# A redesigned order for a gated attention and mixture-of-experts block, without filler products

## The reference

```python
x = x + tanh(g_xattn[0]) * xattn(layernorm(x), ctx_768, Wq, bq, Wkv, bkv, Wo, bo)    # 16 heads of 8
x = x + tanh(g_ffn[0]) * ffn(layernorm(x), Wg, bg, W1, b1, W2, b2)
# ffn: cur = x (2048 tokens); for r in range(4):
    logits = flat @ Wg[r] + bg[r]
    vals, idx = jax.lax.top_k(logits, 2)          # of 4 experts
    w = jax.nn.softmax(vals, axis=-1)
    hmid = jax.nn.gelu(jnp.einsum('nh,ehf->enf', flat, W1) + b1[:, None, :])   # f = 512
    y = jnp.einsum('enf,efh->enh', hmid, W2) + b2[:, None, :]
    cur = cur + einsum('ne,enh->nh', cw, y)       # cw: w at the chosen experts, 0 elsewhere
```

## Time and profile before

| | |
|---|---|
| three runs, us | 505.62 (median), 504.99, 509.12 |
| profiled execution, us | 505.52 |
| its span, us | 503.7 |
| TensorE busy | 479.5 us, 95% of the span |
| VectorE, ScalarE, GpSimd busy | 74%, 75%, 16% |
| chain that ended last | 83% TensorE, 8% VectorE, 3% ScalarE |
| mean granted clock of TensorE | 0.993 |

### The profile page before, as it was taken

One profiled execution on the slowest core, in us unless ns is written; L12 is line 12 of the kernel. 1 busy time (PEld: TensorE's weight loads), 2 busy tenths in 40 slices (PEclk: granted clock), 3 DMA queues, 4 the chain that ended last, 5 costly groups with the idle time before them and its releaser, 6 DMA issues.

```text
span 503.7 us, 9018 instructions
## 1 busy us (share of the span) xinstructions
PE 479.5 (95%) x2977; PEld 385.5 (77%) x2977; DVE 374.3 (74%) x741; ACT 375.9 (75%) x757; POOL 83.1 (16%) x132
## 2 busy tenths in 40 slices
PE   4798998999999999999999999999999999999995
PEld 3567776777887878888888888888888888888884
DVE  5449587888879687866977697778669776877775
ACT  2457576776969687887878788878878877888773
POOL 5736298673220000000000000000000000000000
PEclk9999799999999999999999999999999999999999
DMA  5900000001302020040031004000400130050001
GB/s 145 320 29 7 10 3 14 2 15 32 139 1 85 0 85 2 3 167 1 1 115 55 0 2 169 1 0 3 167 1 0 44 128 1 0 191 0 21 1 42
DMA packets 15156, 25.20 MB, mean 50 GB/s; under 512 B 3490, under 2 KB 11527, under 8 KB 13063
## 3 DMA queue, kind: packets, MB, share of 16 engines
q1 hardware_dynamic: 11136, 22.05, 12.3%
q0 software_dynamic: 2592, 2.10, 2.3%
q10 hardware_dynamic: 1382, 0.49, 0.4%
HBM read 22.82 MB, written 1.18 MB: 48 GB/s over the span
## 4 chain that ended last, share of the span: by engine, by line
PE 83%; DVE 8%; issue 4%; ACT 3%; DMA 1%; ACTq 1%; DVEq 0%
PE ps L1215 11%; PE ps L1217 11%; PE ps L1216 11%; PE ps L1202 11%; PE ps L1204 11%; PE ps L1203 11%; PE ps L1117 4%; PE ps L1105 3%; PE ps L1133 2%; PE ps L1138 2%; DVE least L800 1%; PE ps L1177 1%; DVE rT_sb L816 1%; PE ps L1176 1%; ACT g_sb L724 1%
## 5 line engine op out<-in xcount | busy, mean ns | idle before, releaser
L851 DVE TENSOR_TENSOR h_lo<-g_sb,h_hi 128x512 fp32r<-128x512 f32 x256 | 170.1, 688 | 78.1 <-ACT h_hi L731 78.1
L724 ACT ACTIVATE g_sb<-ps,cols 128x512 f32<-128x512 f32 x256 | 174.8, 686 | 68.1 <-PE ps L1204 67.8
L731 ACT ACTIVATE h_hi<-g_sb 128x512 fp32r<-128x512 f32 x256 | 154.1, 631 | 0.0
L1215 PE MATMUL ps<-h_hi,w_hi 128*128 128x512 f32 x256 | 103.1, 403 | 0.0
L1217 PE MATMUL ps<-h_hi,w_lo 128*128 128x512 f32 x256 | 101.2, 395 | 0.0
L1202 PE MATMUL ps<-x_hi,w_hi 128*128 128x512 f32 x256 | 101.1, 395 | 0.0
L1216 PE MATMUL ps<-h_lo,w_hi 128*128 128x512 f32 x256 | 101.0, 394 | 0.0
L1204 PE MATMUL ps<-x_hi,w_lo 128*128 128x512 f32 x256 | 100.1, 391 | 0.0
L1203 PE MATMUL ps<-x_lo,w_hi 128*128 128x512 f32 x256 | 99.8, 390 | 0.0
L1217 PEld LDWEIGHTS ps<-h_hi,w_lo 128*128 128x128 f32 x256 | 48.0, 188 | 11.9
L1204 PEld LDWEIGHTS ps<-x_hi,w_lo 128*128 128x128 f32 x256 | 48.0, 188 | 11.3
(11 more groups left out here) (122 smaller groups left out, 480.0 us busy)
## 6 DMA issues: line engine op xcount, KB each, us to landing
cwb_even<-cw_rows SPq DMA_DIRECT2D x8, 1024.0 KB, 5.0
cwb_odd<-cw_rows SPq DMA_DIRECT2D x8, 1024.0 KB, 4.7
w_hi<-in_L_ffn_W_dram POOLq DMA_DIRECT2D x2, 1024.0 KB, 9.1
x_sb<-in_x_dram SPq DMA_DIRECT2D x4, 256.0 KB, 5.2
w_in<-in_L_ffn_W_dram SPq DMA_DIRECT2D x1, 1024.0 KB, 6.2
out_dram<-xn SPq DMA_DIRECT2D x4, 256.0 KB, 2.3
ctx_sb<-in_ctx_dram ACTq DMA_DIRECT2D x4, 115.5 KB
v_st<-v_sb SPq DMA_DIRECT2D x8, 38.5 KB
```

The source lines that it names most:

```text
L724: nc.scalar.activation(g_sb[:, k, :], ps[:, k, :], ACT.Gelu_apprx_tanh, bias=b1_c[:, e * NF + k:e * NF + k + 1]).then_inc(gelu_done, 1)
L731: nc.scalar.activation(h_hi[:, u % 2, k, :], g_sb[:, k, :], ACT.Copy).then_inc(hi_done, 1)
L851: nc.vector.tensor_tensor(h_lo[:, u % 2, k, :], g_sb[:, k, :], h_hi[:, u % 2, k, :].bitcast(F32), ALU.subtract).then_inc(lo_done, 1)
L1215: mm(yb, w2_hi[:, w], hh, start=k == 0, stop=False)
```

## The change

Six things change. Shown are the parts that decide an order; the rest follows from them.

The router's logits of the six paired routes are made from the other side: the router weights are now the stationary operand (`wg_w`: four copies of high and low part in 32-column groups, made once by VectorE in batch 3), x moves past them in four products of 512 columns (`wide_logits`), ScalarE copies the 8 useful rows of each group to `lgs` (`move_logits`), and one unit later two transposes bring them to tokens by columns. Ranking, weights and transposed weights come one unit later, the gate in the same unit as before.

```diff
         LOGITS_AT = {1: 2, 5: 3}
         ROUTER_AT = {2: 2, 6: 3}
         GATE_AT = {2: 2, 6: 3}
         WEIGHTS_AT = {3: 2, 7: 3}
-        CWT_AT = {4: 2, 8: 3}
-        MOVE_AT = {4: 2, 8: 3}
+        CWT_AT = {5: 2, 8: 3}
+        MOVE_AT = {5: 2, 8: 3}
         for q in range(NC, len(ROUTES)):
             u = 2 * E * (q - NC + 1)
-            LOGITS_AT[u + 1] = q
-            ROUTER_AT[u + 2] = q
+            WIDE_AT[u + 1] = q
+            LOGITS_AT[u + 2] = q
+            ROUTER_AT[u + 3] = q
             GATE_AT[u + 3] = q
-            WEIGHTS_AT[u + 3] = q
-            CWT_AT[u + 5] = q
-            MOVE_AT[u + 5] = q
+            WEIGHTS_AT[u + 4] = q
+            CWT_AT[u + 6] = q
+            MOVE_AT[u + 6] = q
...
+            def wide_logits(q):
+
+                pe.wait_ge(wg_split, 4)
+                pe.wait_ge(x_split, ROUTES[q][-1] + 1)
+                pe.wait_ge(gate_step, GATE_OPS * (q - 1) + 2)
+                pe.wait_ge(cwT_moved, q)
+                wg = wg_w[:, ROUTES[q][0] // NC, :, :].rearrange("p t w -> p (t w)")
+                for n, i in enumerate(ROUTES[q]):
+                    mm(ps[:, 6 + n, :], wg, x_hi[:, i % NC, :], start=True, stop=False)
+                    m = mm(ps[:, 6 + n, :], wg, x_lo[:, i % NC, :], start=False, stop=True)
+                m.then_inc(lgw_done, 1)
+
+            def transpose_logits(q):
+
+                k = 32 * (TC - 1) + 2 * E
+                pe.wait_ge(lgw_moved, q - NC + 1)
+                for n in range(2):
+                    m = tr(ps[:, 6, n * P:n * P + k], lgs[0:k, n, :], ident[0:k, 0:k])
+                m.then_inc(logits_done, 1)
+
...
+            def move_logits(q):
+
+                act.wait_ge(lgw_done, q - NC + 1)
+                act.wait_ge(zero_done, 2)
+                if q > NC:
+                    act.wait_ge(logits_done, q - 2)
+                for t in range(TC):
+                    rows = slice(32 * t, 32 * t + 2 * E)
+                    m = nc.scalar.activation(lgs[rows, :, :], ps[rows, 6:8, t * P:(t + 1) * P], ACT.Copy)
+                m.then_inc(lgw_moved, 1)
+
```

At the start the first chunk is split into a part "a" (batch 0) and "b" (batches 1 to 3), the low and high K of batch 0 are made on VectorE (`stage_k0`), and GpSimd issues its two large loads ahead of the inverse deviations. TensorE, VectorE and GpSimd:

```diff
-            transpose_xn(0)
+            transpose_xn("a")
             moved(pe, "W")
             project_k(0)
             moved(pe, "W")
+            project_q("a")
+            moved(pe, "W")
             project_v(0)
+            scores(0, 0)
+            scores(0, 1)
+            transpose_xn("b")
             moved(pe, "W")
-            project_q(0)
+            project_q("b")
             pe.wait_ge(bv_wide, 1)
             mm(bank("BO")[:, 0:D], bv_w[:, :], wT[:, 3, :], start=True, stop=True).then_inc(job_mm, 1)
-            scores(0, 0)
-            scores(0, 1)
...
-            moments(0, 0)
             dve.wait_ge(c_ready, 2)
             nc.vector.tensor_reduce(head_mask[:, :], head_at[:, :, :].rearrange("p q h -> p h q"), AX.X,
                                     ALU.add).then_inc(headmask_ready, 1)
-            normalise(0)
-            moments(0, 1)
-            normalise(1)
+            moments(0, "a")
+            normalise("a")
+            moments(0, "b")
+            stage_k0()
             moved(dve, "COLS")
-            low_q(0)
+            low_q("a")
+            normalise("b")
             smallest(0, 0)
             shift(0)
+            moments(0, 1)
             smallest(0, 1)
+            moved(dve, "COLS")
+            low_q("b")
+            normalise(1)
...
-            rstd_of(0, 0)
-            rstd_of(0, 1)
+            pool.wait_ge(headmask_ready, 1)
             pool.dma_start(w1_hi[:, :].rearrange("h (e f) -> h e f", e=E),
                            W1.rearrange("e h f -> h e f")).then_inc(w_hi, 16)
             pool.dma_start(w2_hi[:, :].rearrange("p (e k h) -> p e k h", e=E, k=NF),
                            W2.rearrange("e (k p) h -> p e k h", p=P)).then_inc(w_hi, 16)
-            pool.wait_ge(headmask_ready, 1)
-            stage_k(0)
+            rstd_of(0, "a")
+            rstd_of(0, "b")
             stage_k(1)
+            rstd_of(0, 1)
```

```diff
-        NORMALISE = {3: 2, 7: 3}
+        NORMALISE = {4: 2, 8: 3}
...
                     smallest(b + 1, 0)
+                if c < NC and r == R_LOW:
+                    low_q(c)
                 if b + 1 < B:
                     shift(b + 1)
                 if b >= 2:
                     normalise_o(b - 2)
-                if b == ROUTER1_SLOT:
-                    router(1)
-                if c < NC and r == R_LOW:
-                    low_q(c)
+                if b in SPLIT_X:
+                    split_x(SPLIT_X[b])
                 if b == ROUTER0_SLOT:
                     router(0)
-                if b + 1 < B:
-                    smallest(b + 1, 1)
                 if b == WEIGHTS0_SLOT:
                     weights(0)
                 if b in NORMALISE:
                     normalise(NORMALISE[b])
+                if b == ROUTER1_SLOT:
+                    router(1)
+                if b + 1 < B:
+                    smallest(b + 1, 1)
                 if b in MOMENTS:
                     moments(*MOMENTS[b])
-                if b in SPLIT_X:
-                    split_x(SPLIT_X[b])
                 if b == 3:
                     dve.wait_ge(moe_ld, 16 * 4)
                     nc.vector.tensor_copy(wg_s[:, :, 0, :], wg_in[:, :, :]).then_inc(wg_split, 1)
                     dve.wait_ge(wg_split, 1)
                     nc.vector.tensor_tensor(wg_s[:, :, 1, :], wg_in[:, :, :], wg_s[:, :, 0, :].bitcast(F32),
                                             ALU.subtract).then_inc(wg_split, 1)
+                    dve.wait_ge(zero_done, 2)
+                    wg_t = wg_in[:, :, :].unsqueeze(2).to_broadcast([P, ROUNDS, TC, E])
+                    nc.vector.tensor_copy(wg_w[:, :, :, 0:E], wg_t).then_inc(wg_split, 1)
+                    dve.wait_ge(wg_split, 3)
+                    nc.vector.tensor_tensor(wg_w[:, :, :, E:2 * E], wg_t, wg_w[:, :, :, 0:E].bitcast(F32),
+                                            ALU.subtract).then_inc(wg_split, 1)
```

At the end, the last unit's `down`, `share`, `add_share`, the transposes, `finish` and the store are split into halves of 256 tokens (`down_half` has 12 products of 256 columns):

```diff
-                down(u)
-            transpose_cur(NC - 1)
+                if u + 1 < UNITS:
+                    down(u)
+            down_half(0)
+            down_half(1)
+            transpose_cur_half(0)
+            transpose_cur_half(1)
...
-            add_share(UNITS - 1)
-            finish(NC - 1)
+            share_half(0)
+            add_half(0)
+            share_half(1)
+            add_half(1)
+            finish_half(0)
+            finish_half(1)
```

More of the change, by code:

```diff
@@ L457, in _ @@
                 spread_weights(q)
-            for c in range(NC):
+            for c in range(NC - 1):
                 sp.wait_ge(fin_done, c + 1)
@@ L561, in _ @@
             for b in range(B):
+                add_bias(b)
                 if b in POOL_LN:
@@ L1078, in project_q @@
                 moved(pe, ("XN", c))
-                mm(bank(key), wT[:, 0, :], xnT[:, c % 2, :], start=True, stop=True).then_inc(job_mm, 1)
+                g, at = batches(c)[0] // TC % 2, columns(c)
+                mm(bank(key)[:, at], wT[:, 0, :], xnT[:, g, at], start=True, stop=True).then_inc(job_mm, 1)
             def project_v(c):
```

244 lines of the change are left out of this document (173 added, 71 removed).

## The result

The changed kernel takes **488.61 us** (median of 4 executions, 488.21 to 488.88) against 507.19 of the kernel before (4 executions, 504.99 to 509.12): ratio 0.963, 95% interval 0.959 to 0.968. The direction was forecast, the size was not: 494.8 with a range of 491 to 501. Between the two profiled executions, 505.52 and 488.53 us, the gain is 17.0 us instead of 10.7.

What follows compares the result with a forecast made beforehand. TensorE was taken to bound the feed-forward part, with waits and a lower-clock stretch in the attention. From 505.5 us the terms -2.9 - 1.0 - 2.7 - 1.0 - 3.0 + 1.0 - 1.1 = -10.7 gave 494.8 us, range 491 to 501.

Steps and rivals of the forecast that it cites:

- (a): Router logits of the six paired routes: four wide products and two transposes replace 16 narrow products, -2.9 us for six.
- rival three: Paired units: ScalarE's gate waits for the later ranking, with 3.2 us in hand; if missed, +3, 497.8 us; chance 0.09.
- (b): Weights of route 2 transposed a unit later, so TensorE no longer stands 1.03 us for `cw`: -1.0 us.
- (c): Attention: VectorE's normalisations move behind the residual add; three of TensorE's four waits for `x_sb` go, -2.7 us.
- (d): Attention: ScalarE takes probabilities ahead of K and Q results; a third of TensorE's 2.9 us wait goes, -1.0 us.
- (e): Attention, 49 to 56 us: the fall to the lower clock goes with the stall in batch 3, -3.0 us.
- Rival one: Attention: the clock falls somewhere else, so the clock term becomes 0 to +1: 497.8 us; chance 0.20.
- (f): Start: POOL's two large loads delay the first `xn`, and everything after waits for the whole chunk again: +1.0 us.
- Rival two: Start: the clock's higher level comes a batch or more later; one batch later gives 497.8 us; chance 0.14.
- (g): End: last chain in halves, about 1.9 us instead of 3.0, with more second-layer products and a smaller last transfer: -1.1 us.

Runs made afterwards that it cites:

- b_order: Kernel before with only the order of ScalarE and TensorE in the attention batches taken from the changed kernel: 502.5 us, ratio 0.989.
- a_loads: Changed kernel with POOL's two large loads behind the first 1/sigma instead of ahead of it: 488.8 us.
- a_logits: Changed kernel with the narrow logits of the six paired routes, ranked a unit earlier as before: mean of three executions 492.7 us.
- a_norm: Changed kernel with only VectorE's normalisations moved back to batches 3 and 7: 497.7 us.
- a_norm_rep: a_norm with the transposes of the context in batches 4 and 8 made three times, to fill part of the stall: 492.5 us.
- a_vec: Changed kernel with all of VectorE's old table in the attention batches: 495.4 us.
- b_norm: Kernel before with only VectorE's four normalisations one batch later: 506.9 us, ratio 0.995.
- a_order: Changed kernel with the old order of ScalarE and TensorE in the attention batches: 496.5 us.
- a_fill: Changed kernel with 27 transposes of the identity in TensorE's waits of the first 19 us: 485.3 us.
- best1: a_fill with two more waits of the start filled, 7 products each: 483.4 us, ratio 0.952 to the kernel before.

## Why the prediction was right or wrong

**(a) Paired logits, -2.9, measured -3.9: right, undersized.** The step that was too large was 0.28 us for the two transposes. The second layer starts 0.12 us behind the first of them (271.20 to 271.32), where I had taken 0.14 for each. The 0.14 came from the length of a row of eight, which holds the modelled end of the last; by the starts eight cost 0.96 us (44.16 to 45.12 before), 0.12 each. So the pair costs 0.12 instead of 0.28, and that is all of the 0.16 us by which a round was better than forecast (46.35 to 45.70 is 0.65, not 0.49). The copies on ScalarE (1.52 us) were hidden, and ScalarE's wait for the ranking came nearly as worked out, 3.54 us against 3.8. TensorE did not stand for it (45.70 us busy of 45.70), so the 3.2 us in hand were enough, and rival three fell.

**(b) Route 2, -1.0, measured -1.37: right.** No idle time ahead of its transpose: 1.03 us of the 1.37 are idle time, as forecast, and the other 0.34 busy time that nothing here explains. Route 3, which was not moved, still shows 0.3 us.

**(c) and (d), -2.7 and -1.0, together -3.7, measured -5.9: the step that failed.** By the waits after 32 us, (c) was about right: TensorE's waits for `x_sb` went from 3.3 to 0.9 us, 2.4 for 2.7. (The four splits took 1.7 us, from 43.61 to 45.27, not 2.8.) It is (d) that was undersized: the waits for `probT` at L1117, 2.9 us, all went, where I had taken a third of them because a wait in a chain through three engines usually reappears in part. b_order shows that the argument was right for that edit alone: 2.9 us went and 2.6 came back as a wait for the low half of Q. What the prediction left out is that VectorE's table, in the same change, puts `low_q` ahead of the shift and so takes away the place where the wait would reappear. About 0.6 us more are short gaps that no row of the waits names: TensorE was idle for 8.1 us after 32 us (84.31 busy in 92.39), of which the two rows that I priced from hold 6.2.

**(e) The clock, -3.0, measured -5.0 in busy time: right in kind, undersized, and in part luck.** The stretch lasted 6.8 us, from 49.4 to 56.2, and at half the clock that is worth 3.4 at most. Busy time in the ruler fell by 3.95 us for the same 1013 records; the other 0.5 is not attributed. 0.96 us more come from batch 2, where the higher level was reached about a microsecond earlier than in the trace of before. Another 0.11 is at the seam. The sum had nothing for batch 2, and its gain can't be put down to the change: a_loads and a_logits have the same program of TensorE there, and in their profiles the higher level came about 1 us and about 5 us later than in the changed kernel's. That TensorE's standing still has a part in the fall is now shown by a_norm and a_norm_rep; that it is enough is not, by a_vec. The Trainium skill (TensorE: Matmul & The Clock Gate, Part 1) says that a block of the chip sets TensorE's clock by how busy that engine has been; the runs agree, with a granted clock of 0.51 behind the stall of 1.32 us and 1.00 where it was filled. Rival one (the clock falls elsewhere) did not come in the changed kernel, but in kernels that keep more of the idle time it did: in b_norm, a_order and a_vec.

**The base.** The sum was made from one execution of 505.5 us, which looked like the median of three. Over the 48 executions that ran beside the experiments, 16 lie at 504.8 to 505.8 and 31 at 507.9 to 510.3, and one at 514.5: the median is 508.5. So part of the gain in the median is a spread of the old kernel that the forecast did not count. The 3.5 us between the two groups are near the price of one stretch at the lower level, but their mean granted clocks overlap (0.970 to 0.993 and 0.964 to 0.984), so that this is what parts them is not shown.

**(f) The start, +1.0, measured +0.54: right in sign, for a reason half wrong.** POOL's issues do lie ahead of the first `xn` (7.64), but not on the path. K's projection, copy and staging end at 12.19, and a_loads moved `xn` by 2.0 us for nothing. The second scores came at 19.69, inside 19.5 to 20.5; the loss is the rest of the chunk, as the second half of the step said. Rival two fell: eight transposes take 1.12 us by 33.

**(g) The end, -1.1, measured -1.3: right.** The half products cost 0.3 us more, as forecast (-15.61 at the last unit's first layer, -15.31 at its last product): their starts are 0.124 us apart in the mean (479.38 to 482.24 in 23 steps), where I had taken 0.13. From the start of the last product to the issue of the last transfer it is 2.3 us (482.24 to 484.54), before 3.4 (497.55 to 500.99): -1.1, as forecast, though the forecast had 1.9 and 3.0 for the two. The smaller transfer saved 0.45 instead of 0.3. The estimate by the Trainium skill (TensorE: Matmul & The Clock Gate, LDWEIGHTS), 0.107 us a product and -1.6 for the term, was too low a price by that measured spacing.

**In sum:** of the 6.2 us that the forecast lacked, 2.2 are the idle time of (c) and (d), 2.0 the clock of (e), 1.0 of it from batch 2, 1.0 is (a), and 1.0 the three small terms.

## What to carry to other kernels

Before pricing waits, take the bound engine's idle time over the whole stage from its busy time, and make the named waits add up to it; the rest is there to be won or lost too. Where a wait may reappear, name the instruction behind which it would, and look whether the change moves that one as well. Where engines hand data around in a ring, orders that fit pay together and hardly alone, so an edit tried by itself gives no price for it. And a stall of TensorE can cost more than its length: in a_norm one line brought 2.3 us more of idle time in the ruler and 9 us in the median, and needless products in the stalls won back 5.

## What the runs showed of the hardware

The lower level of the clock is not a property of a kernel but of an execution: of the four of a_vec one had a mean granted clock of 0.986 and three 1.00, and the profile shows one sample. Products that nobody reads help to raise the clock: in a_fill eight transposes take 1.12 us at 20.97, where the changed kernel first shows that at 32.39. Transposes alone can do it: in best1 TensorE had run nothing else when the higher level came at about 7 us. Stalls of much the same length (1.31 and 1.32 us, in the same batch of a_vec and a_norm) were followed by no fall and by one. The four normalisations on VectorE took 3.12 us in a_norm, 2.51 in the earlier trace rows and 1.90 in the changed kernel, and a single one between 0.34 and 1.00. In a_norm POOL works beside them from 43.82 us on without a gap; whether that is the cause was not tried.
